# Eight PSUM banks and eight buffer pairs in place of four in the last stage of a window-attention and Fourier-filter kernel

## The chip, the cores and the metric

The kernel runs on one core of one Trainium2 chip. The metric is the device time of one execution in microseconds (us); smaller is better. The kernel before takes 8733.94 us, the median of three executions (8728.36 to 8739.25).

## The reference

The input x has the shape (8, 256, 256, 64): eight images, 256 rows (in the second layer these are the time steps), 256 columns, 64 channels, all float32.

The first layer is a Swin block: attention inside shifted windows of 4 x 4 positions with four heads, a normalisation, an MLP with GELU, and a second normalisation. The second layer filters each channel along the rows:

```
trend = moving_average(x, 25)                       # along the 256 rows
xs = rfft(x - trend, axis=1)[:, :128]
ys = einsum('bmnc,cmk->bknc', xs, w_real + 1j * w_imag)
out = trend + irfft(ys padded with zeros, n=256, axis=1)
```

All of the second layer is linear along the rows. For one channel c it is therefore one 256 x 256 matrix applied to the 256 rows of each image, the same matrix for all eight images. The kernel builds these 64 matrices first, and its last stage multiplies them by the output of the first layer.

## The kernel before

The program has three parts, one after the other, each engine with its own stream of instructions.

**Part 1, the matrices.** For each of the 64 channels TensorE multiplies the weights by constant DFT matrices, and the result (128 x 512 float32, 256 KB) goes to the DRAM tensor `mix`. This part uses the buffers `amat[0]` and `amat[1]` as a place to store from.

**Part 2, the Swin block.** It walks over 512 groups of 16 x 32 pixels and takes most of the time (up to about 7470 us of the trace). It writes its result to the DRAM tensor `y`, laid out as (image, row, channel, column). Nothing of this part is touched by the change. At its end all engines have finished with all eight PSUM banks, because `y` must be complete before part 3 reads it (L366, L722, L916).

**Part 3, the last stage.** It loops over the eight images (`b` in the code), and for each over 64 channels. One channel of one image is:
- SyncE (SP) issues two loads (`channel_in`, L371 to L377): the matrix of the channel from `mix` into `amat[j]` (256 KB, as 128 rows of 2 KB), and the channel's 256 rows of `y` into `xch[j]` (256 KB, as 256 rows of 1 KB). Both count up the semaphore `ch_in[j]`.
- TensorE (`channel`, L575 to L584) waits for `ch_in[j]`, and for PSUM bank `j` to have been copied out, and runs four float32 matmuls with 256 columns into bank `j`. The profile shows them as eight matmul instructions and eight weight loads. The last one counts up `o_ps`.
- ScalarE (`put`, L716 to L719) copies the bank to the SBUF tile `orow` for even channels, VectorE (L910 to L913) for odd ones. `orow` is the whole of `arena`, 128 KB per partition, and holds one image's output: 128 partitions x 2 x 256 x 64 values, with the channel innermost.

The buffer number is `j` = channel modulo `NB`, and `NB` is 4. SP reissues into buffer `j` when `o_ps` says that the matmuls of the channel `NB` before have finished. So at most four channels lie loaded or on their way, and at most four banks hold results that are not yet copied out.

After the 64th channel of an image, ScalarE waits for all 64 copies (L729, L730) and issues four stores of 4 MB each to `out` from its own DMA queue (L733). `orow` is there only once. So ScalarE and VectorE wait for the four stores to land (`rows_out`, L725 and L919) before they copy the first channel of the next image. TensorE and SP do not wait for the stores directly: they go on into the next image until the banks or the buffers are used up. There are eight images, so seven such boundaries and one last store at the end.

The last store of an image is issued from ScalarE's DMA queue (q10 in the profile), the loads from SP's (q1). Both run on the same 16 DMA engines.

Of the kernel before, what the change touches and what calls it, by code (L numbers as in the profile page):

```python
# [84 lines left out]
def swin_then_fourier(nc, x, qkv_wt, qkv_b, v_b, proj_wt, proj_b, logit_scale, cpb_w1t, cpb_b1, cpb_w2t,  # L85
# [6 lines left out]
    BL1, NCH = out.shape[0], C  # L92
# [4 lines left out]
    with ExitStack() as ctx:  # L97
        def sb(name, cols):
            return ctx.enter_context(nc.sbuf_tensor(name, [P, cols], F32))

        def sem(name):
            return ctx.enter_context(nc.semaphore(name))
# [56 lines left out]
        ystripe = [sb(f"ystripe{i}", ROWS * HALF)[:, :].rearrange("p (r q n) -> p r q n", r=ROWS, q=GPS)  # L159
                   for i in range(2)]  # L160

        NB = 4
        dftm, invm, avgm = sb("dftm", 1024), sb("invm", 512), sb("avgm", 512)
        wri = [sb(f"wri{i}", 2 * P) for i in range(2)]
        vri = [sb(f"vri{i}", 512) for i in range(2)]
        amat = [sb(f"amat{i}", 512) for i in range(NB)]
        xch = [sb(f"xch{i}", 512) for i in range(NB)]
        orow = arena[:, :].rearrange("p (k n c) -> p k n c", k=2, c=C)
# [46 lines left out]
        v_ps, v_sb, m_ps, m_sb = sem("v_ps"), sem("v_sb"), sem("m_ps"), sem("m_sb")  # L215
        m_out = [sem(f"m_out{i}") for i in range(NB)]
        ch_in = [sem(f"ch_in{i}") for i in range(NB)]
        o_ps, o_act, o_dve, rows_out = sem("o_ps"), sem("o_act"), sem("o_dve"), sem("rows_out")
# [54 lines left out]
        def _(sp):  # L273
# [97 lines left out]
            def channel_in(b, cq, j, before):  # L371
                if before is not None:
                    sp.wait_ge(o_ps, before)
                c = cq * NB + j
                sp.dma_start(amat[j][:, :], mix[bass.ds(c, 1)].rearrange("a p n -> (a p) n")).then_inc(ch_in[j], 16)
                sp.dma_start(xch[j][:, :].rearrange("p (k n) -> p k n", k=2),
                             y[b].rearrange("(k t) c n -> t k c n", k=2)[:, :, bass.ds(c, 1), :].rearrange("t k c n -> t k (c n)")).then_inc(ch_in[j], 16)  # L377

            for b in range(BL1):
                for j in range(NB):  # L380
                    channel_in(b, 0, j, b * NCH + j + 1 - NB if b else None)
# [6 lines left out]
        def _(pe):  # L388
# [186 lines left out]
            def channel(b, cq, j, first):  # L575
                pe.wait_ge(ch_in[j], cq * 32 + (b * (NCH // NB) + 1) * 32)
                if not first:
                    pe.wait_ge(o_dve if j % 2 else o_act, cq * 2 + (b * (NCH // 2) + j // 2 - 1))
                for k in range(2):
                    for r in range(2):  # L580
                        ins = mm(ps[:, j, k * T:(k + 1) * T], amat[j][:, r * T + k * P:r * T + (k + 1) * P],  # L581
                                 xch[j][:, r * T:(r + 1) * T], start=(r == 0), stop=(r == 1))
                ins.then_inc(o_ps, 1)

            for b in range(BL1):
                for j in range(NB):
                    channel(b, 0, j, b == 0)
                with pe.Fori(1, NCH // NB) as cq:
                    for j in range(NB):
                        channel(b, cq, j, False)  # L590
# [3 lines left out]
        def _(act):  # L594
# [121 lines left out]
            def put(b, cq, j):  # L716
                act.wait_ge(o_ps, cq * NB + (b * NCH + j + 1))
                f(orow[:, :, :, bass.ds(cq * NB + j, 1)].rearrange("p k n c -> p (k n) c"),  # L718
                  ps[:, j, :].unsqueeze(2), ACT.Copy).then_inc(o_act, 1)  # L719
# [3 lines left out]
            for b in range(BL1):  # L723
                if b:
                    act.wait_ge(rows_out, 64 * b)  # L725
                with act.Fori(0, NCH // NB) as cq:
                    for j in (0, 2):
                        put(b, cq, j)
                act.wait_ge(o_dve, (b + 1) * NCH // 2)  # L729
                act.wait_ge(o_act, (b + 1) * NCH // 2)  # L730
                for k in range(2):
                    for hh in range(2):
                        act.dma_start(out[b, k * P:(k + 1) * P, hh * 128:(hh + 1) * 128, :].rearrange("t n c -> t (n c)"),  # L733
                                      orow[:, k, hh * 128:(hh + 1) * 128, :].rearrange("p n c -> p (n c)"))\
                            .then_inc(rows_out, 16)
# [4 lines left out]
        def _(dve):  # L740
# [169 lines left out]
            def put(b, cq, j):  # L910
                dve.wait_ge(o_ps, cq * NB + (b * NCH + j + 1))
                dve.tensor_copy(orow[:, :, :, bass.ds(cq * NB + j, 1)].rearrange("p k n c -> p (k n) c"),  # L912
                                ps[:, j, :].unsqueeze(2)).then_inc(o_dve, 1)  # L913
# [3 lines left out]
            for b in range(BL1):  # L917
                if b:
                    dve.wait_ge(rows_out, 64 * b)  # L919
                with dve.Fori(0, NCH // NB) as cq:  # L920
                    for j in (1, 3):
                        put(b, cq, j)


# [135 lines left out]
```

## Time and profile before

| | us |
|---|---|
| median of three executions | 8733.94 |
| the three | 8739.25, 8733.94, 8728.36 |
| span of the profiled execution, first to last instruction | 8718.4 |
| its own device time | not listed apart from its span |
| start of the last stage's loads (L375) | 7475.93 |
| from there to the end of the span | 1242.5 |
| TensorE busy / ScalarE busy / VectorE busy over the span | 93% / 70% / 69% |

The median is 15.5 us above the span. A row with an engine name is a group of its instructions; `PEld` is TensorE's weight load, which overlaps the matmuls, and a name that ends in q (SPq, ACTq) is that engine's instruction queue, where it issues DMAs. L581 is the line of the matmuls of the last stage, L718 ScalarE's copy, L912 VectorE's copy, L375 and L376 the two loads, L733 the stores.

### The profile page before, as it was taken

The page shows a single profiled execution, that of the slowest core. Times are in us where ns is not written, and L with a number is a line of the kernel's source. Part 1 is how long each engine was busy: PE and PEld are TensorE (multiplying, and loading weights), DVE is VectorE, ACT ScalarE, POOL GpSimd, SP SyncE. Part 2 cuts the span into 40 slices and gives each one's busy share as a digit, 9 for nine tenths or more (in the row PEclk, how much of TensorE's full clock was granted, in tenths as well). Part 3 has the DMA queues.
Part 4 walks back from the last instruction along what each step waited for, and adds up shares of the span by engine and source line. Part 5 has one row for each costly group of instructions (what it writes and reads, how often), then busy time and mean ns, then how long its engine had stood idle before and what let it go on. Part 6 is the DMA issues. An engine that isn't in the chain of part 4 may idle for free.

```text
span 8718.4 us, 659317 instructions
## 1 busy us (share of the span) xinstructions
PE 8075.8 (93%) x293684; PEld 5336.5 (61%) x293684; DVE 5980.8 (69%) x8029; ACT 6123.3 (70%) x8530; POOL 5386.1 (62%) x5127
## 2 busy tenths in 40 slices
PE   8899999999999999999999999999999999778686
PEld 5556666666666666666666666666666666566565
DVE  1467878877878888887888777888877787222121
ACT  1478888888888888888888888888888888322121
POOL 0367777777777777777777777777777777000000
PEclk9799999999999999999999999999999999889898
DMA  3122222222222222222222222222222222799999
GB/s 99 51 50 56 58 57 57 56 58 58 57 57 57 58 57 57 56 57 57 55 55 58 58 57 56 58 58 57 57 57 58 57 57 54 240 315 322 332 319 334
DMA packets 1187111, 834.30 MB, mean 96 GB/s; under 512 B 633233, under 2 KB 1043217, under 8 KB 1182867
## 3 DMA queue, kind: packets, MB, share of 16 engines
q1 hardware_dynamic: 1182404, 698.61, 31.2%
q10 hardware_dynamic: 4608, 134.22, 3.6%
q8 instruction: 80, 1.31, 0.1%
q14 instruction: 19, 0.16, 0.0%
HBM read 412.97 MB, written 285.21 MB: 80 GB/s over the span
## 4 chain that ended last, share of the span: by engine, by line
PE 69%; ACT 13%; issue 13%; DMA 4%; SPq 0%; ACTq 0%; DVE 0%; POOL 0%; POOLq 0%; DVEq 0%
PE ps L479 15%; PE ps L554 11%; PE ps L581 10%; PE ps L501 8%; PE ps L526 6%; PE ps L513 6%; PE ps L462 5%; ACT L705 4%; PE ps L450 4%; ACT arena L653 4%; DMA out<-arena 3%; ACT arena L688 3%; ACT arena L682 2%; PE ps L424 1%; ACT arena L671 1%
## 5 line engine op out<-in xcount | busy, mean ns | idle before, releaser
L479 PEld LDWEIGHTS ps<-arena 32*32 32x32 f32 x131072 | 1259.2, 106 | 710.3 <-issue 686.6
L953 POOL TENSOR_TENSOR arena<-arena 128x512 f32<-128x512 f32 x1024 | 1043.7, 1040 | 898.3 <-PE ps L501 898.3
L479 PE MATMUL ps<-arena 32*32 32x16 f32 x131072 | 1370.2, 180 | 189.3 <-ACT arena L653 164.8
L501 PEld LDWEIGHTS ps<-arena 32*32 32x32 f32 x131072 | 1293.3, 103 | 287.2 <-issue 260.2
L501 PE MATMUL ps<-arena 32*32 32x16 f32 x131072 | 1422.7, 186 | 22.5 <-issue 21.5
L985 POOL TENSOR_TENSOR arena<-arena 128x512 f32<-128x512 f32 x512 | 713.7, 1394 | 861.2 <-DVE arena L844 861.2
L805 DVE TENSOR_TENSOR arena<-ps,arena 128x768 f32<-128x768 f32 x1024 | 980.1, 957 | 370.6 <-PE ps L462 370.5
L581 PE MATMUL ps<-xch,amat 128*128 128x256 f32 x4096 | 923.0, 389 | 288.3 <-ACT arena L718 210.3
L462 PEld LDWEIGHTS ps<-arena 64*128 64x128 f32 x8192 | 648.4, 188 | 837.9 <-issue 830.8
L694 ACT ACTIVATE arena<-ps,arena 128x1024 f32<-128x1024 f32 x1024 | 1130.9, 1105 | 5.1 <-PE ps L542 5.0
L581 PEld LDWEIGHTS ps<-xch,amat 128*128 128x128 f32 x4096 | 787.1, 195 | 424.7 <-ACT arena L718 216.3
L542 PE MATMUL ps<-arena 64*128 64x512 f32 x4096 | 1028.4, 619 | 3.1 <-ACT arena L682 2.3
L554 PE MATMUL ps<-arena 128*64 128x512 f32 x4096 | 1000.6, 608 | 5.0 <-ACT arena L694 4.1
L462 PE MATMUL ps<-arena 64*128 64x192 f32 x8192 | 953.4, 352 | 5.5 <-DVE arena L805 3.2
L718 ACT ACTIVATE arena<-ps 128x512 f32 x256 | 270.7, 1065 | 937.4 <-PE ps L581 608.4
L912 DVE COPY arena<-ps 128x512 f32 x256 | 267.6, 1051 | 942.1 <-PE ps L581 624.9
L877 DVE SCALAR_TENSOR_TENSOR arena<-arena 128x512 f32<-128x512 f32 x512 | 838.6, 1638 | 20.5 <-PE ps L542 20.5
L836 DVE TENSOR_TENSOR arena<-ps,arena 128x512 f32<-128x512 f32 x512 | 354.0, 691 | 722.2 <-PE ps L479 722.2
L991 POOL TENSOR_TENSOR arena<-arena 128x512 f32<-128x512 f32 x512 | 841.7, 1644 | 0.1
L944 POOL TENSOR_TENSOR arena<-arena 128x512 f32<-128x512 f32 x512 | 535.9, 1047 | 276.3 <-ACT arena L622 272.7
L665 ACT ACTIVATE arena<-ps,arena 128x512 f32<-128x512 f32 x512 | 351.8, 687 | 502.3 <-PE ps L530 499.4
L1008 POOL TENSOR_TENSOR ystripe<-arena 128x512 f32<-128x512 f32 x512 | 669.6, 1308 | 12.0 <-DVE arena L889 12.0
(89 smaller groups left out, 14240.3 us busy)
## 6 DMA issues: line engine op xcount, KB each, us to landing
arena<-in_x SPq DMA_DIRECT2D x4096, 32.0 KB
arena<-arena SPq DMA_DIRECT2D x1024, 128.0 KB
y<-ystripe SPq DMA_DIRECT2D x256, 512.0 KB
amat<-mix SPq DMA_DIRECT2D x512, 256.0 KB, 3.3
xch<-y SPq DMA_DIRECT2D x512, 256.0 KB, 4.0
out<-arena ACTq DMA_DIRECT2D x32, 4096.0 KB, 27.6
mix<-amat SPq DMA_DIRECT2D x64, 256.0 KB, 2.0
wri<-in_w_real SPq DMA_DIRECT2D x64, 64.0 KB, 1.8
```

Source lines behind the costliest of these rows:

```text
L462: ins = mm(M[:, a, pl * 256:pl * 256 + 3 * C], xT[a * C:a * C + C, 2 * pp + pl, :], wqkv[a * C:a * C + C, :], start=True, stop=True, tile_ ...
L479: ins = mm(S(sl)[r, c0 + e:c0 + 32:2], qT[r, sl, q, e:64:2], kT[r, sl, q, e:32:2], start=True, stop=True, tile_position=(32 * cg, 32 * cg))
L501: ins = mm(PV[32 * h:32 * h + 32, b, c0:c0 + N], vexp[r, sl, h, :, :], pT[r, sl, h // 2, h % 2, :], start=True, stop=True, tile_position=( ...
L542: ins = mm(M[:, a, :], w1[a * C:a * C + C, kk * P:(kk + 1) * P], x1T[a * C:a * C + C, :], start=True, stop=True, tile_position=(a * C, 0))
L554: ins = mm(H2[a * C:a * C + C, :], w2[:, kk, :], hT[kk][:, a, :], start=(kk == 0), stop=(kk == 1), tile_position=(0, a * C))
L581: ins = mm(ps[:, j, k * T:(k + 1) * T], amat[j][:, r * T + k * P:r * T + (k + 1) * P], xch[j][:, r * T:(r + 1) * T], start=(r == 0), stop= ...
L694: f(hT[kk], M, ACT.Gelu, bias=b1[:, kk:kk + 1]).then_inc(done, 1)
L805: tt(qkv[ring(g, 4)][:, :, 4 * pp:4 * pp + 4, :].rearrange("p w s n -> p s w n"), M.rearrange("p a (s n) -> p (a s) n", s=2)[:, :, 0:3 * C ...
L877: stt(x1T, dn1, g1, xTo[ring(g, 4)], ALU.mult, ALU.add).then_inc(x1_sb, 1)
L953: tt(vexp.rearrange("p s h e d -> p (s h) e d")[:, :, e, :], qkv[ring(g, 4)][:, 2].rearrange("p s (h d) -> p (s h) d", h=HEADS), par[:, e: ...
L985: tt(pr, pr, mx.rearrange("p (n e) -> p n e", e=2).unsqueeze(2).to_broadcast([P, N, N, 2]), ALU.subtract).then_inc(shifted, 1)
L991: tt(pr, pr, rs.rearrange("p (n e) -> p n e", e=2).unsqueeze(2).to_broadcast([P, N, N, 2]), ALU.mult).then_inc(probs, 1)
```

## The change

`NB` becomes 8. With it, eight pairs `amat`, `xch` are allocated in SBUF, eight semaphores each for `ch_in` and `m_out` exist, and the last stage uses PSUM banks 0 to 7. The loops over channels run 8 times over 8 channels in place of 16 times over 4. TensorE's wait for the copy of its bank counts four copies per engine and round in place of two. SP's waits on `o_ps` follow from `NB` without an edit: buffer `j` is loaded again when the channel eight before has been computed. `orow`, the stores, the work of one channel and its order are unchanged.

```diff
-        NB = 4
+        NB = 8
...
             def channel(b, cq, j, first):
                 pe.wait_ge(ch_in[j], cq * 32 + (b * (NCH // NB) + 1) * 32)
                 if not first:
-                    pe.wait_ge(o_dve if j % 2 else o_act, cq * 2 + (b * (NCH // 2) + j // 2 - 1))
+                    pe.wait_ge(o_dve if j % 2 else o_act, cq * (NB // 2) + (b * (NCH // 2) + j // 2 + 1 - NB // 2))
...
                 with act.Fori(0, NCH // NB) as cq:
-                    for j in (0, 2):
+                    for j in range(0, NB, 2):
                         put(b, cq, j)
...
                 with dve.Fori(0, NCH // NB) as cq:
-                    for j in (1, 3):
+                    for j in range(1, NB, 2):
                         put(b, cq, j)
```

## Rows read from the trace of the kernel before

**Rows 1.** The page: span, and the DMA engines' busy tenths in 40 slices.
```profile
span 8718.4 us, 659317 instructions
...
DMA  3122222222222222222222222222222222799999
```

**Rows 2.** The page's groups: line, engine, tiles, count | busy, mean ns | idle before, releaser.
```profile
L581 PE MATMUL ps<-xch,amat 128*128 128x256 f32 x4096 | 923.0, 389 | 288.3 <-ACT arena L718 210.3
...
L718 ACT ACTIVATE arena<-ps 128x512 f32 x256 | 270.7, 1065 | 937.4 <-PE ps L581 608.4
```

**Rows 3.** The chain that ended last, in order of time: start, us, what.
```profile
7597.05 42.39 DMA out<-arena
7639.70 1.30 ACT arena L718
7641.04 78.86 PE ps L581 x352
7719.91 28.10 PE ps L581 x128
7750.06 1.37 ACTq L733
7751.46 43.80 DMA out<-arena
...
8568.60 1.30 ACT arena L718
```

**Rows 4.** Who waited for whom, 7480 to 8719: total us, times, longest.
```profile
PE ps L581 <- ACT arena L718: 210.3, 7, 40.2
PE ps L581 <- DMA xch<-y: 77.7, 8, 15.6
```

**Rows 5.** Timeline of TensorE alone, 7590 to 7645: start, us, instructions, idle before.
```profile
7589.83 9.01 PE L581 MATMUL ps<-xch,amat 128*128 128x256 f32 x41
7608.46 3.78 PE L581 MATMUL ps<-xch,amat 128*128 128x256 f32 x8 [9.61 <-DMA xch<-y]
7641.04 4.25 PE L581 MATMUL ps<-xch,amat 128*128 128x256 f32 x10 [28.80 <-ACT arena L718]
```

**Rows 6.** Timeline of all engines at the same boundary, 7576 to 7660.
```profile
7593.81 1.04 DVE L912 COPY arena<-ps 128x512 f32 x1 [2.42 <-PE ps L581]
...
7594.88 3.44 ACTq L733 DMA_DIRECT2D out<-arena  x4
...
7612.42 3.09 SPq L375 DMA_DIRECT2D amat<-mix  x1
7615.70 9.82 SPq L376 DMA_DIRECT2D xch<-y  x1
```

**Rows 7.** Two of ScalarE's copies, 50 channels apart in one image.
```profile
7658.79 1.05 ACT L718 ACTIVATE arena<-ps 128x512 f32 x1 [2.30 <-PE ps L581]
...
7746.49 1.05 ACT L718 ACTIVATE arena<-ps 128x512 f32 x1 [2.50 <-PE ps L581]
```

**Rows 8.** DMA, 7595 to 7640, a store's time: packets, MB, share; issues: count, KB, landing.
```profile
q10 hardware_dynamic: 576, 16.78, 87.5%
q1 hardware_dynamic: 1595, 2.02, 12.9%
...
xch<-y SPq DMA_DIRECT2D x4, 256.0 KB, 40.6
```

**Rows 9.** DMA, 7755 to 7785, inside the next store.
```profile
q10 hardware_dynamic: 423, 12.29, 95.2%
q1 hardware_dynamic: 423, 0.54, 4.9%
```

**Rows 10.** DMA, 7660 to 7720, between stores.
```profile
q1 hardware_dynamic: 14228, 17.92, 93.5%
...
xch<-y SPq DMA_DIRECT2D x34, 256.0 KB, 4.0
```

**Rows 11.** Busy by stretch, 7482 to 7484: PE, PEld, DVE, ACT, POOL, clock, DMA share, GB/s.
```profile
7482.00:7484.00 2.00, 2.00 (x6) 1.55 (x6) 0.00 (x0) 0.69 (x1) 0.00 (x0) 0.50 1.01 365
```

## The prediction

> **What bounds the kernel now.** I began with the page's 40 slices: the change touches only the last stage, and the DMA slices show where that is, the last six, where the DMA engines go from two tenths busy to seven and nine [rows 1]. So two resources are near their limit in this stage, TensorE and the DMA engines. The groups of the stage come next: TensorE's matmuls are busy 923.0 us and idle 288.3 us, while ScalarE's copy is busy 270.7 us in the whole stage and waits 608.4 us for the matmuls [rows 2]. The copies are therefore never the bottleneck as such. The chain of waits then shows the cycle of one image [rows 3]: the four stores of the finished image (42.39 us), one copy (1.30), then 352 and 128 matmuls in a row (78.86 + 28.10 = 106.96 us for 480 matmuls, 60 channels), the last copy, the issue of the next stores (1.37), and the next stores (43.80). The chain's first copies of an image stand at 7639.70 and 8568.60, six cycles apart [rows 3], so a cycle is 928.90 / 6 = 154.8 us.
>
> 60 channels and not 64 is the point. While the stores run, nobody may copy into the output tile; TensorE goes on only until its four banks are full. The view of waits says it in total: 7 waits for ScalarE's copy, 210.3 us, and 77.7 us for loads of rows [rows 4]. The timeline of TensorE shows one boundary [rows 5]: it works until 7598.84, waits 9.61 us for a load, runs eight matmuls (one channel, 3.78 us, at the slow clock: after such idle time the granted clock is 0.50, as in [rows 11]), and then stands 28.80 us until ScalarE's copy has freed a bank. The stores were issued at 7594.88, just after the last copy at 7593.81 [rows 6].
>
> **The change part by part.**
>
> *Eight banks.* TensorE can compute eight channels of the next image before it must wait for a copy, four more than before. These four leave the stretch behind the store. Their price is the pace of a channel there: two of ScalarE's copies 50 channels apart start at 7658.79 and 7746.49 [rows 7], which is 87.70 / 50 = 1.754 us per channel. Four channels are 7.02 us per boundary, and there are seven boundaries: 49.1 us. The first channel after the store still starts at the slow clock, as now (106.96 us for 60 channels is 1.7 us more than 60 x 1.754), so that loss stays.
>
> Is there room for the four in the store's time? From the end of the third channel at 7598.84 to the restart at 7641.04 are 42.2 us [rows 5]; four channels at full clock take 7.0, at the slow clock 15.1 (4 x 3.78). Both fit. The wait for the copy doesn't vanish, it shrinks: what is late next at the restart is again ScalarE's first copy, behind the store.
>
> *Eight pairs of buffers.* TensorE can use the banks only if the channels are loaded. Between stores a load of rows lands 4.0 us (median) after its issue [rows 10]. With eight pairs it is issued eight channels, 14 us, ahead, so at the start of the store all but the last one or two of channels 0 to 7 have landed. Inside the store it is very different: the four loads issued there take 40.6 us (median) to land [rows 8]. The 9.61 us wait [rows 5] is for the fourth channel, whose load was caught half done by the store; now the eighth channel has that place. Its load would land at the same 7608.46, TensorE reaches it at about 7598.84 + 7.02 = 7605.9, and the wait becomes about 2.6 us. Either way all eight are done by about 7612, 29 us before the restart. If a backlog leaves one of the eight loads over to the end of the store, one channel (1.75 us, 12 us over seven boundaries) of the gain goes; none of the eight would be a loss against today.
>
> *Does the store get longer?* After the change eight loads instead of four want to be served during the store. In 30 us in the middle of a store both queues moved the same number of packets, 423 and 423, though the stores' are 29 KB each and the loads' 1.3 KB [rows 9]. So while both have work, the loads get one small packet per large one, 4.9% of the engines' time. The loads already have work for the whole store today: SP's last issue of a load was held up for 9.82 us until 7625.5 [rows 6], and the loads landed only at its end. More loads behind them don't change the alternation. I take 0 for the store's lengthening; the bounds are 0 and the full data of four more loads, 4 x 0.524 = 2.10 MB at the 428 GB/s of that stretch (12.83 MB in 30 us [rows 9]) = 4.9 us per boundary. I take the end at 0 because the row measures the case itself, a load queue with a backlog.
> The Trainium skill, page "DMA: Bandwidth & Descriptors", section "Queues, rings and completion order", says that each DMA engine takes turns between the queues that have work and changes only at a packet's end, a packet being typically 9 to 17 descriptors. The turn taking is what the 423 to 423 show; if a turn of the load queue carried 9 to 17 of the profile's packets, the added loads would fit into the store and lengthen it, which is the second rival below. The counts of the row speak against that.
>
> *The loads after the store.* Here the change costs something new. All but about 3.9 loads of an image (2.02 MB moved in 45 us [rows 8], at 0.524 MB each) must be moved outside the store: 60.1 loads or 31.5 MB, today in 154.8 - 45 = 109.8 us, after the change in 102.8 us. That needs 307 GB/s. Between stores the DMA engines now move 17.92 MB in 60 us, 299 GB/s, at a share of 93.5% [rows 10], paced by TensorE. At a full share it would be 299 / 0.935 = 319 GB/s, an estimate; a stretch with four loads queued shows 365 GB/s at a share of 1.01 [rows 11]. So the DMA engines just carry it, with 4% to spare, because now they need not stand half idle after the restart as buffers are always free for them. I take 0, with a cost of up to 2.8 us per boundary if they can't go above today's 299 GB/s (first rival).
>
> *The rest.* Loops of 8 rounds in place of 16, other thresholds in the waits, more code, more semaphores: nothing is added per channel on any engine. ScalarE and VectorE have 270.7 us of work in a stage of 1242 us [rows 2], so they hide whatever their loop costs or saves. After the store they drain eight banks, four each at about 1.2 us, 5 us, while TensorE needs the second bank only after the first slow channel, so no new wait there. At the start of the stage SP issues eight loads in place of four in a row, but TensorE's first one is first in the queue. I take 0 for all this, within plus or minus 3 us. The end (last copy, last store) is untouched.
>
> *Sum.* Against the profiled execution's span: 8718.4 - 49.1 = 8669.3 us. Its device time isn't listed apart; the median is 15.5 us above its span, so the prediction is 8733.9 - 49.1 = 8684.8, taken as 8685 us.
>
> **The rivals.**
>
> 1. *The DMA engines become the bound between stores.* If their rate doesn't rise above 299 GB/s with deeper buffers, the 60.1 loads take 105.4 us and a cycle is 150.4 us in place of 154.8: a gain of 4.4, less whatever the tail of the store takes, call it 4.2 us per boundary, 29 us in all, 8705 us. For it: the required 307 is above any long stretch of loads alone in this trace, and "93.5% busy" needn't mean that 100% is to be had. Against it: the 365 GB/s of the short stretch, and that TensorE hardly waits for loads outside the stores (77.7 us, in 8 waits, the longest 15.6 [rows 4], about one per boundary).
>
> 2. *The store gets longer.* If the four added loads are all served within it, it costs 4.9 us per boundary and leaves 7.0 - 4.9 = 2.1 us: 15 us in all, 8719 us. For it: all queues share the same engines, which are full there. Against it: the equal packet counts [rows 9].
>
> 3. *The change does nothing.* If at the store's start only the first four channels were loaded, TensorE would stop after them as before: 8734 us. It would take loads that are not issued early, though nothing else than a free buffer and SP's turn holds them; the 4.0 us to landing [rows 10] speaks against it.
>
> 4. *Slower: more loads in flight make each load dearer.* Up to eight loads queue at once after each store, twice as many as now. If their mutual disturbance lowers the rate between stores, the point from which it decides is the rate at which the cycle is again 154.8 us: 31.5 MB in 109.8 us, 287 GB/s, 4% under today's 299. At 275 GB/s (8% under) the cycle is 45 + 114.6 = 159.6 us, 4.8 us more, 34 us in all: 8768 us. For it: the loads have rows of 1 KB and the engines are close to full, so a small loss would tell. Against it: with four loads queued at the start of the stage the rate was higher, not lower [rows 11].
>
> **How the numbers follow.** The forecast, the whole gain or all but one channel of it, gets 0.74, with its own range from 8676 to 8698. Rival 1 gets 0.12, rival 2 0.06, rival 3 0.04 and rival 4 0.04. The range from 8676 to 8712 takes in the forecast and rival 1 and leaves the other three out, 0.14, and a little beyond its ends. What a measurement of this kernel can tell from no change is 0.2%, 17.5 us. Faster by more than that are the forecast and rival 1: 0.86. Within it are rivals 2 and 3: 0.10. Slower is rival 4: 0.04.
>
> **What would show it.** Right: in the chain of waits each image but the first has 448 matmuls (56 channels) and about 100 us in place of 480 and 107; TensorE's timeline has eight channels between the issue of the stores and the restart; its waits for ScalarE's copy and for loads fall together from 288 to about 240 us; the cycle is 147.8 us. The stores still take 42 to 44 us in the chain, which is rival 2's test: 47 to 49 would make it right. For rivals 1 and 4 it is the rate between stores and TensorE's waits for loads there: many small waits and a pace above 1.754 us per channel would show them. If less than four added channels run within the store at a pace that is unchanged, the prefetch failed (rival 3, or the lost channel in the forecast's own range).

## The result, and the profile after

The changed kernel takes 8674.91 us (median of four, 8672.51 to 8683.84) against 8732.2 us for the kernel before (median of four, 8728.36 to 8739.25; three of the four gave the 8733.94 further up): a ratio of 0.993, 95% interval 0.9917 to 0.9942, 57.3 us less. Forecast were 8685 us and a gain of 49.1 us, with a range from 8676 to 8712. The sign was right, and the part that was priced, four more channels inside each store, is in the trace; the gain is 8 us larger, because a part that was put at nothing gave 7.7 us, and the time lies 1 us outside the range.

The span of the profiled execution is 8681.7 us, only 36.7 us under the one before. That isn't the change: the loads of the last stage start at 7496.2 us in this execution and at 7475.9 us in the other, and no instruction ahead of that point does other work. In the profiled executions of the eleven experiments that point lies between 7467.8 and 7491.1 us. So the last stage is read by itself, from the first load to the end of the span: 1242.4 us before, 1185.4 us after, 57.0 us less, close to the 57.3 between the medians.

First the page's groups of the changed kernel, which answer to [rows 2]:

```profile
L581 PE MATMUL ps<-xch,amat 128*128 128x256 f32 x4096 | 914.5, 388 | 240.1 <-ACT arena L718 193.0
...
L718 ACT ACTIVATE arena<-ps 128x512 f32 x256 | 272.2, 1085 | 879.2 <-PE ps L581 551.1
```

TensorE's idle time fell by 48.2 us (288.3 to 240.1), almost the forecast's 49.1. But its busy time fell too, by 8.5 us, with the same 4096 matmuls. That is the part that was not forecast, and it is hidden in a column that is easily read as a constant: short waits inside a run of matmuls are counted as busy. The records of two matmuls overlap (each lasts some 380 ns, and the next starts 216 ns behind it), so a wait of 0.2 us leaves no idle time between them.

The chain in order of time, against [rows 3] (start us, us, what):

```profile
7499.78 112.83 PE ps L581 x512
7614.71 1.32 ACTq L733
7616.06 42.63 DMA out<-arena
7658.95 1.30 ACT arena L718
7660.30 98.98 PE ps L581 x448
7761.33 1.31 ACTq L733
7762.68 42.63 DMA out<-arena
```

Each image after the first has 448 matmuls in the chain in place of 480, 56 channels behind the store, and 99.0 us in place of 107.0. The stores still take 42.6 us.

TensorE alone around the same boundary, against [rows 5]:

```profile
7604.67 20.02 PE L581 MATMUL ps<-xch,amat 128*128 128x256 f32 x92
7633.62 3.69 PE L581 MATMUL ps<-xch,amat 128*128 128x256 f32 x8 [8.94 <-DMA xch<-y]
7660.30 7.88 PE L581 MATMUL ps<-xch,amat 128*128 128x256 f32 x26 [22.99 <-ACT arena L718]
```

The last copy of the image ended at 7613.8. TensorE goes on until 7624.7, seven channels into the next image. It waits 8.94 us for the eighth, whose load was issued at 7613.0, just ahead of the stores, and landed at 7633.6; then it waits 22.99 us for ScalarE's first copy.

Who waited for whom in the last stage, the kernel after (total us, times, longest), against [rows 4]:

```profile
PEld ps L581 <- ACT arena L718: 196.9, 7, 34.2
PE ps L581 <- ACT arena L718: 193.0, 7, 33.8
PEld ps L581 <- DMA xch<-y: 50.4, 7, 15.5
PE ps L581 <- DMA xch<-y: 47.1, 7, 14.6
```

and the same view's lines for TensorE's weight loads in the kernel before, which the prediction had not looked at:

```profile
PEld ps L581 <- ACT arena L718: 216.3, 12, 40.6
PEld ps L581 <- DMA xch<-y: 73.3, 33, 16.0
PEld ps L581 <- issue: 9.3, 39, 0.4
```

The matmul rows of before name 8 waits for loads [rows 4]; the weight loads name 33, most of them under half a microsecond, and 39 more that are put down to issue. After the change TensorE has seven waits for a copy, one per boundary, and seven for loads, the first of them at the start of the stage; no short one is left. The weight loads between two stores show it, first before, then after:

```profile
7665.40 15.41 PEld L581 LDWEIGHTS ps<-xch,amat 128*128 128x128 f32 x72 [0.22 <-DMA xch<-y]
7681.14 17.13 PEld L581 LDWEIGHTS ps<-xch,amat 128*128 128x128 f32 x80 [0.34 <-issue]
7698.64 6.77 PEld L581 LDWEIGHTS ps<-xch,amat 128*128 128x128 f32 x32 [0.36 <-ACT arena L718]
```

```profile
7665.00 89.98 PEld L581 LDWEIGHTS ps<-xch,amat 128*128 128x128 f32 x417
```

Whatever the view names behind these short waits, each of the three ends with a load: the channels' rows of `y` landed at 7665.35, 7681.03 and 7698.52.

The loads and stores of the kernel after inside a store (7620 to 7650), and the loads between stores (7665 to 7755), against [rows 9] and [rows 10] (packets, MB, share):

```profile
q10 hardware_dynamic: 426, 12.39, 96.0%
q1 hardware_dynamic: 423, 0.54, 4.9%
```

```profile
q1 hardware_dynamic: 21871, 27.59, 95.0%
```

Inside a store the loads' line is that of before to the digit, and the stores' differs by under 1% (423 packets, 12.29 MB, 95.2% before). Between stores the loads now move 27.59 MB in 90 us, 307 GB/s in place of 299.

**Where the 57 us came from**, worked out from the starts of the 512 copies in each trace. "Gap" is from an image's last copy to the next image's first; "1 to 64" from an image's first copy to its last, mean of the seven images behind a boundary; "pace" is the mean distance of two copies from the 21st to the 64th of an image; "cycle" is from first copy to first copy, mean of six.

| kernel | device us | ratio to before, 95% | stage | cycle | gap | 1 to 64 | pace |
|---|---|---|---|---|---|---|---|
| before | 8732.2 | | 1242.4 | 154.8 | 46.3 | 108.4 | 1.747 |
| changed | 8674.9 | 0.993 (0.9917 to 0.9942) | 1185.4 | 146.7 | 46.2 | 100.6 | 1.727 |

From 1 to 64 it is 7.82 us less (108.39 to 100.57), seven times: 54.7 us. Of that 4 x 1.727 = 6.91 us, 48.4 in all, are the four channels that are now done inside the store. The other 6.3 us, and 1.4 us of the first image, are the pace. The gap gives 0.8 us. Together 56.9 us.

The pace can be followed to the single load. Take the 352 channels from the 21st of each image on. Before the change the load of a channel's rows was issued 4.3 us before the channel's first matmul and landed 4.0 us after its issue (medians). In 146 of the 352 the first weight load starts within 0.13 us of the landing of its own load, which is to say that it waited for it; 48 of these channels come late by more than 0.03 us, and the 146 together lose 6.8 us against 1.727 us per channel. The other 206 lose nothing. In the changed kernel a load is issued 11.2 us ahead and lands at least 5.8 us before its first weight load, and no channel is late.

### The profile page after: what moved, and what is told of

Read it like the earlier page. It is cut to its first block, busy times and chain, and to the rows that moved or that the text cites. A ratio compares the mean times of both kernels' runs of the same rounds, so it can differ in the third digit from the quotient of the medians.

```text
span 8681.7 us, 658585 instructions
## 1 busy us (share of the span) xinstructions
PE 8078.5 (93%) x293684; PEld 5352.2 (62%) x293684; DVE 5975.8 (69%) x8029; ACT 6127.7 (71%) x8530; POOL 5385.9 (62%) x5127
## 4 chain that ended last, share of the span: by engine, by line
PE 68%; ACT 13%; issue 13%; DMA 4%; SPq 1%; ACTq 0%; DVE 0%; POOL 0%; POOLq 0%; DVEq 0%
PE ps L479 15%; PE ps L554 11%; PE ps L581 9%; PE ps L501 8%; PE ps L526 6%; PE ps L513 6%; PE ps L462 5%; ACT L705 4%; PE ps L450 4%; ACT arena L653 3%; DMA out<-arena 3%; ACT arena L688 3%; ACT arena L682 2%; PE ps L424 1%; ACT arena L671 1%
## 5 line engine op out<-in xcount | busy, mean ns | idle before, releaser
L581 PE MATMUL ps<-xch,amat 128*128 128x256 f32 x4096 | 914.5, 388 | 240.1 <-ACT arena L718 193.0
L813 DVE TENSOR_REDUCE arena<-arena 128x64 f32<-128x1024 f32 x512 | 624.5, 1220 | 85.0 <-ACT arena L629 68.8
```

## The experiments

The kernel before was timed beside each group of experiments: 8739.1 us for e1 to e4, 8722.7 us for e5 to e8, 8736.4 us for e9 to e11. Ratios are to that. The stage is from one trace per kernel; the two traces of the changed kernel (this one's 1185.4 and e9's 1187.2) are 1.8 us apart, so a difference of 2 us in that column says nothing.

| kernel | device us | ratio to before, 95% | stage | cycle | gap | 1 to 64 | pace |
|---|---|---|---|---|---|---|---|
| e1, 8 pairs, 4 banks | 8731.2 | 0.9992 (0.9983 to 1.0001) | 1238.6 | 154.1 | 46.5 | 107.7 | 1.727 |
| e2, 4 pairs, 8 banks | 8728.8 | 0.9988 (0.9979 to 0.9997) | 1232.8 | 153.3 | 46.1 | 107.3 | 1.750 |
| e3, loops of 8 alone | 8745.0 | 1.0007 (0.9998 to 1.0016) | 1246.9 | 155.2 | 46.1 | 109.3 | 1.752 |
| e4, 16 pairs, 8 banks | 8683.5 | 0.9939 (0.9926 to 0.9953) | 1187.0 | 146.8 | 46.4 | 100.5 | 1.727 |
| e5, loads withheld from the 9th | 8667.3 | 0.9936 (0.9921 to 0.9952) | 1185.1 | 146.7 | 44.2 | 102.6 | 1.727 |
| e6, joined loads | 8692.2 | 0.9967 (0.9955 to 0.9979) | 1211.7 | 150.2 | 49.1 | 101.1 | 1.727 |
| e7, joined, 16, withheld from the 17th | 8657.3 | 0.9929 (0.9916 to 0.9943) | 1179.6 | 145.9 | 45.0 | 100.8 | 1.727 |
| e8, joined, 16 | 8687.4 | 0.9961 (0.9946 to 0.9977) | 1208.1 | 149.6 | 48.7 | 101.0 | 1.727 |
| e9, changed kernel again | 8675.8 | 0.993 (0.9917 to 0.9944) | 1187.2 | 146.9 | 46.2 | 100.6 | 1.727 |
| e10, joined, 16, withheld from the 13th | 8650.6 | 0.9901 (0.9886 to 0.9916) | 1158.5 | 142.6 | 41.6 | 101.1 | 1.727 |
| e11, plain, 16, withheld from the 13th | 8654.7 | 0.9908 (0.9893 to 0.9923) | 1162.5 | 143.1 | 42.4 | 101.0 | 1.727 |

### Which part of the change does it: e1, e2, e3

In all of these the numbers of load pairs, of banks and of channels per loop round are separate:

```diff
-        NB = 8
+        NBUF, NBANK, UNR = 8, 4, 8      # e1; e2: 4, 8, 8; e3: 4, 4, 8
...
+                i = j % NBUF
...
-                        ins = mm(ps[:, j, k * T:(k + 1) * T], amat[j][...], xch[j][...], ...)
+                        ins = mm(ps[:, j % NBANK, k * T:(k + 1) * T], amat[i][...], xch[i][...], ...)
```

> Eight pairs of load buffers, but only four PSUM banks, channel loops of eight. Theory A (the four channels per image boundary need free banks; and beside it the deeper loads remove small waits for loads in the stretch between stores, which is the part the forecast missed): the boundary keeps its 60 channels after the store, the pace falls from 1.745 to 1.727 us per channel, so the last stage loses 60 x 0.018 = 1.1 us per image, 8 to 10 us in all: a stage of 1233 us against 1242.5, about 8723 us. Rival B (buffers alone are what counts, banks hardly): most of the 57 us, about 8680. Rival C (the small waits come from the banks): no change, 8732.

> Eight PSUM banks, but only four pairs of load buffers, channel loops of eight. Theory A: at the store's start four channels are loaded; the loads of the next four are served at one small packet per large store packet and land near the store's end, so at most one more channel runs before the restart: 0 to 4 us per boundary, pace unchanged at 1.745, between 8705 and 8732 us. Rival (banks alone are enough): eight channels before the restart, 49 us less, 8684.

> Four banks and four pairs as before; only the channel loops have eight channels per round in place of four. Theory A (small waits are for loads): nothing changes, pace 1.745 us, stage 1242 us, 8732 us. Rival D (the turn of the loop costs TensorE time every four channels): the pace falls toward 1.736 or less, the stage by 4 to 9 us, 8724 to 8728.

e1: the pace fell to 1.727, the boundary kept its four channels, and theory A holds; rival B (buffers alone) and rival C (the small waits come from the banks) are out. The gain was smaller than expected: 3.8 us in the stage, 7.9 us in the medians (the interval just reaches no change). Against e3, which has the same loops and differs in the pairs alone, the stage is 8.3 us shorter. From 1 to 64 it is 0.7 us per image and not 1.1. The waits of TensorE in e1 (L582 is its line of the matmuls):

```profile
PEld ps L582 <- issue: 290.6, 7, 43.6
PE ps L582 <- ACT arena L719: 288.0, 7, 43.2
PEld ps L582 <- DMA xch<-y: 15.4, 1, 15.4
```

The many short waits are gone (the one wait for a load is the start of the stage). At a boundary there is one long wait of 41.1 us in the mean (288.0 / 7), for a bank alone, where before there were two.

e2: eight banks with four pairs bring 9.6 us in the stage, inside the expected 0 to 28. TensorE's waits and one boundary:

```profile
PE ps L582 <- DMA xch<-y: 256.3, 19, 28.6
```

```profile
7739.69 19.82 PE L582 MATMUL ps<-xch,amat 128*128 128x256 f32 x90
7769.17 3.78 PE L582 MATMUL ps<-xch,amat 128*128 128x256 f32 x8 [9.67 <-DMA xch<-y]
7799.81 20.52 PE L582 MATMUL ps<-xch,amat 128*128 128x256 f32 x84 [26.85 <-DMA xch<-y]
```

The boundary looks like that of before, but the last wait ends with a load and not with a copy: TensorE has free banks and nothing to put into them. Alone the two halves of the change give 3.8 and 9.6 us in the stage (8.3 and 14.1 against e3), together 57.0. A load issued before the store is worth a channel only if a bank is free for it, and the reverse.

e3: no gain (the stage is 4.5 us longer, the ratio's interval holds 1). Rival D, by which longer loops save time, is out. Why the stage is a little longer was not followed up; its pace, 1.752, is that of a few more late loads. TensorE's weight loads in e3 still have their short waits:

```profile
PEld ps L582 <- issue: 197.0, 53, 29.7
PEld ps L582 <- DMA xch<-y: 102.9, 35, 16.3
```

### Do more loads in flight cost anything: e4, e5

e4 has sixteen pairs (the added ones in the tiles of part 1 and 2 that are free by then). e5 has eight and one added wait:

```diff
+                if b:
+                    sp.wait_ge(rows_out, 64 * b)     # e5: ahead of the 9th channel's load
```

> Sixteen pairs of load buffers (the added ones lie in tiles that are free in the last stage), eight banks, channel loops of sixteen. Theory A: the banks limit TensorE to eight channels inside a store and nothing waits for loads between stores, so nothing is left to gain: the cycle stays 146.7 us and the stage 1185 us, 8675 us, within 3. The stores, whose packets alternate one to one with the loads', stay at 46.2 us from the last copy to the first. Rival E (more queued loads lengthen a store or make loads dearer): the store grows by up to 10 us, eight more loads of 0.524 MB at 428 GB/s, up to 8745 us.

> The changed kernel, but SP withholds the loads of the ninth and later channels of an image until the stores of the image before have landed, so that no new load competes with a store. Theory A (packets of the two queues alternate, a load packet costs its own small time): the time from an image's last copy to the next image's first falls from 46.2 to about 41 us (the last store of the kernel, with no loads beside it, takes 41.8). But the loads that it displaces come later: 64 loads or 33.6 MB outside the store, at no more than 319 GB/s 105 us, and TensorE waits about 2 us for the ninth channel. Cycle about 147 to 148 us in place of 146.7, 8675 to 8690 us, with many waits for loads between stores. Rival (loads beside a store cost it nothing): the gap stays 46, and the cycle grows to 149 or more, 8695 or above.

e4 came out as theory A has it: cycle 146.8, gap 46.4. Its 8683.5 us lie above the expected 8675, but the kernel before took 8739.1 beside it, so 55.7 us less. Twice the depth neither helps nor lengthens a store.

e5: the gap fell, but by 2.0 us and not by 5, and the stage is that of the changed kernel within 0.3 us, the cycle 146.7. TensorE alone at its first boundary (its first copy of the new image starts at 7641.93):

```profile
7589.73 19.80 PE L584 MATMUL ps<-xch,amat 128*128 128x256 f32 x91
7612.09 1.99 PE L584 MATMUL ps<-xch,amat 128*128 128x256 f32 x8 [2.56 <-DMA xch<-y]
7645.46 4.79 PE L584 MATMUL ps<-xch,amat 128*128 128x256 f32 x13 [31.38 <-DMA xch<-y]
```

The restart waits for the ninth channel's load, 3.5 us behind the first copy, and eats what the shorter gap gave. That the gap stays over 41 us goes with the loads issued just ahead of the stores: TensorE starts on the eighth channel, whose load it waited for, only at 7612.09, 13 us after the stores' issue at 7598.66. Past that wait the loads outside the store did not hold TensorE back: the pace is 1.727. So the part of theory A by which the DMA engines are then too slow failed, and e11 takes it up.

### What a load packet costs a store: e6, e7, e8

The loads of two channels are joined; the matrices lie in DRAM in pairs.

```diff
-                sp.dma_start(amat[j][:, :], mix[bass.ds(c, 1)]...)          # 128 rows of 2 KB
-                sp.dma_start(xch[j][:, :]..., y[b]...[:, :, bass.ds(c, 1), :]...)  # 256 rows of 1 KB
+                sp.dma_start(amat[i][:, :], mix[bass.ds(c, 1)]...)          # two channels, 128 rows of 4 KB
+                sp.dma_start(xch[i][:, :]..., y[b]..."(k t) (c e) n -> t k c (e n)"...[:, :, bass.ds(c, 1), :]...)  # 256 rows of 2 KB
```

> The changed kernel with the loads of two channels joined: the matrices lie in DRAM as 128 rows of 4 KB per pair of channels, the rows of y are read as 256 rows of 2 KB per pair, two DMAs for two channels in place of four. Eight banks, room for eight channels as before. Theory A (between stores TensorE alone sets the pace, 1.727 us per channel, once eight channels are buffered): the DMA engines' share between stores falls from 95% to about 85 to 90%, and the time hardly moves: the gap may grow by 1 us because a load packet beside a store is larger; 8675 us, within 5. Rival (the DMA engines still hold TensorE back somewhere): faster by 5 us or more.

> Joined loads as in e6, room for sixteen channels, eight banks, and no loads of the seventeenth and later channels before the stores of the image before have landed. Theory A: the gap from last to first copy falls to 41 to 43 us, the eight channels behind the restart are already loaded, and the joined loads (under 1.6 us per channel) can be moved beside 56 channels of TensorE's work: cycle 142 to 144 us, 20 to 33 us faster than the changed kernel, about 8650 us. Rival (the loads don't get cheaper by being joined, 105 us per image must follow a 41 us store): cycle 146 to 147, 8675 us.

> As e7, but loads are not withheld during a store. Theory A: gap 46 to 47 us as in the changed kernel, cycle 146 to 147 us, 8675 us within 5; so e7's gain, if there is one, comes from withholding and not from the joined loads or the depth. Rival: it is as fast as e7, then the depth or the joining does it.

e6 was a miss: it is slower than the changed kernel, by 26 us in the stage, not equal. Between stores the joined loads are cheaper, as expected (share 0.90 at 304 GB/s where the changed kernel has 0.95 at 307). But the gap grew by 2.9 us, three times the allowance. Inside one of its stores (7600 to 7630):

```profile
q10 hardware_dynamic: 407, 11.76, 90.8%
q1 hardware_dynamic: 407, 1.01, 8.5%
```

The packets alternate again, 407 to 407, but a load packet is now 2.5 KB in the mean, the loads take 8.5% of the time where they took 4.9%, and the store gets 90.8% where it got 96.0%. e8, with sixteen channels' room, shows the same gap (48.7), so it isn't the depth. It is the one thing in this study that makes a store longer. Seven gaps of 2.9 us are 20.6 of the 26 us; 3.7 us are in the seven times 1 to 64 (101.1 against 100.6), 0.7 in the first image, and 1.2 in the first copy of the stage, which starts 8.64 us behind the first load's issue in place of 7.45.

e7 withholds loads from the seventeenth channel on. The gap fell from e8's 48.7 to 45.0, not to 41 to 43: the last pair's load is still issued just ahead of the stores (at 7593.59, the stores at 7594.41) and lands beside them. Its stage is 5.8 us under the changed kernel's; the rival's "8675" would have been about equal, so neither number was met (on the medians it is 65.4 us under the kernel before of its group, where the changed kernel is 57.3 under its own).

### The version that beats both: e9, e10, e11

```diff
                 for j in range(0, UNR, 2):      # e11: range(UNR), plain loads
+                    if b and j == 12:
+                        sp.wait_ge(rows_out, 64 * b)
                     pair_in(b, 0, j, b * NCH + j + 2 - NBUF if b or j >= NBUF else None)
```

> The changed kernel once more, as the measure for the two beside it on the same chip. Stage 1185 us, cycle 146.7 us, gap from last copy to first copy 46.2 us, about 57 us faster than the kernel before.

> As e7 (joined loads, room for sixteen channels, eight banks), but the loads are withheld from the thirteenth channel of the next image on and not from the seventeenth, so the last load is issued some 8 us before the stores and none is under way beside them. Theory A (the gap is 41.8 us with no load beside the stores, and joined loads reach the 353 GB/s seen behind a restart in e7, so 64 of them or 33.6 MB take 95 us): the gap falls from 45.0 to 41.8 or 42.5, the 56 channels behind the restart still take TensorE's 100.8 us, the cycle is 142.6 to 143.5 us, the stage about 1160 us, some 24 us under the changed kernel. Rival (the stores' time isn't set by the loads left under way): gap 45, cycle 146.

> The same withholding and depth with the plain loads of the changed kernel (256 KB each, 1 KB and 2 KB rows). Theory A (plain loads reach no more than 319 GB/s, the estimate of the prediction, so 33.6 MB take 105 us beside a store of 41.8 us): gap 41.8 to 42.5, but now the DMA engines set the pace behind the restart, with many waits for loads; cycle 146 to 147.5 us, no faster than the changed kernel. Rival (plain loads can go at 350 GB/s too when enough of them are queued): cycle 143, as e10.

e9 repeats the changed kernel: stage 1187.2, ratio 0.993. e10 did what was expected of it: gap 41.6 us, the very time of the kernel's last store, which has nothing beside it (41.8), cycle 142.6, stage 1158.5, 28.7 us under e9. It is the fastest kernel here, 8650.6 against 8675.8 us on the same chip. Its chain (L725 is its copy):

```profile
7611.14 38.47 DMA out<-arena
...
7649.88 1.30 ACT arena L725
7651.31 99.40 PE ps L588 x448
7753.76 38.46 DMA out<-arena
```

The stores take 38.5 us where they took 42.6.

The gaps of six kernels now say what the loads cost a store. With plain loads they are 46.2 us (changed), 44.2 (e5, only the loads issued just ahead left) and 42.4 (e11, none left); with joined loads 48.7 (e8), 45.0 (e7) and 41.6 (e10). The depth doesn't matter to them (46.4 in e4, 49.1 in e6). So the loads issued during the store cost 2.0 us plain and 3.7 joined, those just ahead of it 1.8 and 3.4. The packets give the same for the first pair, by an estimate. The stores of one image are 512 packets of 32 KB, 32 for each of the 16 engines, and each is followed by one load packet, which takes 59 ns in the mean when plain (46 ns for 1 KB, 84 for 2 KB) and 109 ns when joined (84 for 2 KB, 159 for 4 KB): 1.9 us and 3.5 us. How the loads just ahead of a store cost theirs was not traced.

e11 met the rival and not theory A (whose gap alone held, 42.4): plain loads do it nearly as well, cycle 143.1, ratio 0.9908 (e10's interval and its own overlap). Busy time by stretch behind a restart of e11 (after the busy columns of five engines: clock, DMA share, GB/s):

```profile
7655.00:7685.00 30.00, 30.00 (x137) 26.23 (x137) 9.05 (x9) 9.99 (x10) 0.00 (x0) 0.97 1.06 366
7685.00:7745.00 60.00, 60.00 (x280) 52.82 (x279) 18.02 (x18) 18.04 (x18) 0.00 (x0) 1.00 1.04 348
```

Plain loads with a queue behind them move at 366 and 348 GB/s for 90 us, where the prediction's estimate was 319.

## Why the prediction was right or wrong

**Eight banks.** Right. 448 matmuls per image in the chain, eight channels inside the store, the restart still behind ScalarE's first copy. Four channels were priced at 1.754 us from [rows 7]; they cost 1.727, so this term is 48.4 and not 49.1 us.

**Eight pairs of buffers, inside the store.** Right in the place: the eighth channel took over the fourth's wait. Its length was not: 8.94 us at the boundary shown, 2.6 forecast, because the load landed 19.8 us behind the stores' issue and not 13.6 as the fourth's had. That wait doesn't decide anything, since the channel is done 23 us before the restart. e1 and e2 show that neither half works without the other.

**Eight pairs of buffers, between the stores.** This is the step that failed. The prediction gave the deeper buffers no effect there but a possible cost, and under rival 1 it took as evidence "that TensorE hardly waits for loads outside the stores". That came from the matmul rows [rows 4]. The weight loads, which come first in each channel, had 33 waits for loads and 39 called issue. [rows 7] held the trace of it too: 1.754 us per channel was taken as TensorE's own pace, while it was 1.727 plus waits. With four pairs a load had 4.3 us from its issue to its use and took 4.0, so every late one showed, and all of the lost time lies in channels that waited for their own load; with eight pairs it has 11.2 us. e1 (pairs alone) brings the pace to 1.727, e2 (banks alone) and e3 (loops alone) don't. The missed term is 7.7 us, and with 0.8 us of shorter gaps and 0.7 us too much for the banks it makes the difference between 49.1 and 57.0. The cycle is 146.7 us in place of the forecast's 147.8 for the same reason.

**The store's length.** Right: 46.3 and 46.2 us, 42.6 in the chain, and the packets alternate as in [rows 9]; rival 2 is out for this change, and by e4 for twice the depth. The reason given, a queue with a backlog takes its turn and no more, is borne out by e6 from the other side: double the bytes of a turn, and the gap is 2.9 us longer; e10 takes the turns and the loads just ahead away, and it is 4.6 us shorter. Equal counts alone would fit turns of several packets as well, but the packets' times don't: in the changed kernel, from 7620 to 7650, 373 of the 391 load packets of 1 or 2 KB start within 5 ns of the end of a store packet and end within 5 ns of the start of the next. The Trainium skill's rule of turns ("DMA: Bandwidth & Descriptors", section "Queues, rings and completion order") agrees with that; its 9 to 17 descriptors per packet are not seen in the profile's packets, of which one turn of the loads was a single one, 1.3 KB or 2.5 KB in the mean.

**The loads after the store.** The demand was right, 307 GB/s, and met without a wait. The ceiling was wrong: 299 / 0.935 = 319 GB/s took the share for a linear gauge, and e11 ran at 366 and 348. The row of 365 GB/s [rows 11], used only as a support, was the better measure. So rival 1 had less to stand on than its 0.12.

**The range.** Its low end, 8676, allowed 9 us beyond the sum. Between the stores only a cost had been bounded, not a gain, and the missed gain fell out on that side.

**The rest.** Loops and start: e3 shows no gain from the loops. The 15.5 us between median and span were read as what lies around the span. In the runs after, the device time of the profiled execution is 1.8 to 2.2 us above its span; the rest would be an execution faster than the median, and the record has no device time of it. The sum was not touched by it.

## What to carry to other kernels

Buffers ahead of an engine and room behind it are worth something only together when both stall at the same event: count how many units can be both loaded before it and parked behind it, and the smaller count is the gain. Before pricing an engine's pace as its own, look at the waits of the instruction that comes first in each unit (here the weight load): short waits are counted as busy, and here deeper buffers removed them. Compare the time from a load's issue to its use with the time that it takes to land: 4.3 us against 4.0 had no room. Where a large transfer is on the path and small ones aren't, keep the small ones out of its way. Issue them early enough to be done, hold the others back, and let them catch up behind it; that was worth another 25 us here.

## What the runs showed of the hardware that was not expected

- Two DMA queues with work alternated packet by packet at both sizes that were run: 423 to 426 with 29 KB against 1.3 KB, 407 to 407 with 29 KB against 2.5 KB (means). A load issued beside a store then took 40.6 us in place of 4.0 [rows 8, rows 10]. Larger rows in the background transfer slowed the one in front, by 3.7 us in place of 2.0.
- Loads in rows of 1 and 2 KB run at 299 to 307 GB/s at a DMA share of 0.94 to 0.95 when TensorE paces them, and at 366 GB/s at 1.06 with a queue behind them (e11). At 0.95 the share of busy time overstated how near the engines were to their limit.
